# Ternary layer reordered, first normalisations moved a stage ahead, and int8 weights rounded in portions inside the third attention

## The reference

```
x = x + tanh(g_xattn[l]) * xattn_l(layernorm(x), ctx)
x = x + tanh(g_ffn[l])   * ffn_l(layernorm(x))          # l = 0..3
```

```
layer 0: routed, 16 experts, top 6, and a shared expert
layer 1: scale = mean(|w|); w_q = sign(w) * (|w| >= 0.7*scale)   for w1 (1024x256), w2 (256x1024)
         out = gelu(x @ w1_q.T + b1) @ w2_q.T + b2
layer 2: w_scale = max|w| over a row / 127; w_q = clip(round(w / w_scale), -128, 127)
         x_scale = max|x| over a token / 127; x_q likewise
         y = (x_q @ w_q.T) * x_scale * w_scale + bias
layer 3: routed, 8 experts, top 2, and a shared expert
```

## Time and profile before

| | us |
|---|---|
| median of 3 runs | 1062.74 |
| lowest, highest | 1055.58, 1065.13 |
| profiled execution | 1061.1 |
| its span, first to last instruction | 1059.3 |
| PE busy | 912.0 (86%) |
| DVE busy | 579.4 (55%) |
| ACT, POOL busy | 336.6 (32%), 417.2 (39%) |

### The profile page before, as it was taken

The page is one execution under the profiler, slowest core; times in us unless marked ns, Lnnn a source line. Parts: engine busy times, 40 slices in busy tenths (PEclk is TensorE's granted clock), DMA queues, the critical chain, the costliest instruction groups (busy, mean ns, idle before and its releaser), DMA issues. The chain is left out here.

```text
span 1059.3 us, 14410 instructions
## 1 busy us (share of the span) xinstructions
PE 912.0 (86%) x4605; PEld 702.2 (66%) x4605; DVE 579.4 (55%) x1084; ACT 336.6 (32%) x607; POOL 417.2 (39%) x328
## 2 busy tenths in 40 slices
PE   1999999697889999999949966899379788999996
PEld 1888788596656666666838965878257655565664
DVE  5567776555834444442468979666676542222221
ACT  2243443332023333333324324344133331121221
POOL 2477666203058888785322201260070005022222
PEclk9999999796679999999969977899569989899999
DMA  6411210006925544654721010000000095222210
GB/s 249 164 43 48 79 42 1 1 1 221 365 65 86 86 74 75 152 85 89 212 76 44 2 35 1 21 1 2 25 1 1 2 392 228 71 47 37 39 33 11
DMA packets 38432, 84.79 MB, mean 80 GB/s; under 512 B 9709, under 2 KB 27501, under 8 KB 35726
## 3 DMA queue, kind: packets, MB, share of 16 engines
q1 hardware_dynamic: 22190, 64.63, 17.3%
q0 software_dynamic: 16176, 19.31, 11.0%
HBM read 71.23 MB, written 20.68 MB: 87 GB/s over the span
## 5 line engine op out<-in xcount | busy, mean ns | idle before, releaser
L2391 PE MATMUL ffn_GU<-ffn_W,ffn_XTB 128*128 x252 | 91.1, 484 | 1.3 <-DVE ffn_XTB L2300 0.7
L1874 PE MATMUL ffn_GU<-ffn_W,ffn_XTB 128*128 x184 | 85.0, 605 | 0.0
L1694 POOL DMA_INDIRECT out_x<-ffn_YB,ffn_XB x23 | 35.8, 1557 | 120.2 <-DVE ffn_YB L1823 118.2
L2100 POOL DMA_INDIRECT kept_MARKED<-scratch_rows,kept_IDX x63 | 62.6, 994 | 52.0 <-DVE kept_IDX L2277 33.1
L2284 DVE TENSOR_TENSOR ffn_GB<-ffn_GU,ffn_BIAS 128x352 f32<-128x352 f32 x63 | 33.1, 525 | 87.4 <-PE ffn_GU L2391 76.2
L2391 PEld LDWEIGHTS ffn_GU<-ffn_W,ffn_XTB 128*128 128x128 f32 x252 | 43.8, 191 | 33.7 <-issue 19.4
L2422 PE MATMUL ffn_DN<-ffn_W,ffn_HT 96*128 x252 | 64.9, 380 | 0.0
L1901 PE MATMUL ffn_DN<-ffn_W,ffn_HT 128*128 (+1 forms) x248 | 58.8, 380 | 1.9 <-issue 1.2
L1812 DVE COPY ffn_XTB<-ffn_XP 128x256 f32<-128x256 f32 x23 | 9.8, 425 | 89.3 <-PE ffn_XP L1883 89.3
L2140 ACT ACTIVATE ffn_HG<-ffn_GB 128x176 f32<-128x176 f32 x63 | 22.1, 350 | 114.5 <-DVE ffn_GB L2284 81.6
L1874 PEld LDWEIGHTS ffn_GU<-ffn_W,ffn_XTB 128*128 128x128 f32 x184 | 33.1, 189 | 35.9 <-issue 33.4
(11 more groups left out here) (493 smaller groups left out, 2496.6 us busy)
## 6 DMA issues: line engine op xcount, KB each, us to landing
ffn_W<-in_f_w SPq DMA_DIRECT2D x9, 1536.0 KB, 6.6
ffn_W<-in_f_w SPq DMA_DIRECT2D x16, 608.0 KB, 17.6
attn_W<-in_L_pairs SPq DMA_DIRECT2D x8, 1088.0 KB, 4.9
scratch_rows<-in_rows_empty SPq DMA_DIRECT2D x1, 2967.0 KB, 14.2
ffn_XB<-scratch_rows SPq DMA_DIRECT2D x23, 129.0 KB, 2.1
ffn_BIAS<-in_f_bias SPq DMA_DIRECT2D x1, 2816.0 KB, 13.5
kept_STAGE<-in_f_w SPq DMA_DIRECT2D x1, 2048.0 KB, 8.3
kept_STAGE<-in_L_pairs SPq DMA_DIRECT2D x2, 768.0 KB, 5.6
```

The source lines that it names most:

```text
L1694: pool.indirect_dma_start(out[:, :], bass.IndirectOffsetOnAxis(ap=XB[:, i % NB, D:D + 1].bitcast(I32), axis=0), YB[:, i % 3, :], None, bou ...
L1874: last = pe.matmul(GU[:, m, :], x, weights(e, k * 2 * HID3 + m * HID3, HID3), start=k == 0, stop=k == KD - 1)
L2100: pool.indirect_dma_start(XB[:, i % NB, :], None, DR["rows0"][:, :], bass.IndirectOffsetOnAxis(ap=IDX[:, i:i + 1], axis=0)).then_inc(rows_ ...
L2391: last = pe.matmul(GU[:, n % 2, 0:2 * HID], XTB[:, i % 2, k * P:(k + 1) * P], flat[:, bass.ds(e * WIDTH0 + k * 2 * HID, 2 * HID)], start=k ...
```

## The change

Six things are done.

1. **First roots and normalisations in the stage ahead.** `early_root` (ACT, first four tiles) and `early_norm` (DVE, their reciprocal and four normalised tiles, put between the last two `add`) stand at the end of the first attention, `attend`, `ternary` and the third attention. At the end of the fourth attention only the root is taken early, and the int8 layer does the same for it. The following stage does the second half alone (`rooted`, `normalised`).
2. **Sums of |w|** for the ternary layer are taken by ACT inside `attend`, in four portions of 1024 elements in steps 2 to 5.
3. **Ternary layer's start**: thresholds first, LE of the first matrix ahead of the normalisation, the bias B2G ahead of WQT of the first matrix, the second matrix after `vector_low`; PE waits for half of the transposed input only.
4. **Ternary layer's rest**: every third chunk's HS_hi is rounded by ACT (`by_act`), and PE's output tiles are put between the chunks from the tenth on.
5. **Int8 weights**: `int8_weights` loads them with the third attention's first DMAs and quantises them in four portions on DVE, in the steps 5 to 8 of the third attention.
6. **Int8 layer**: weight products and transposes come first on PE, the bias is added to tiles 0 to 3 by DVE and to 4 to 7 by POOL.

```diff
+        def early_root(act, measured, rooted):
+            act.wait_ge(measured, T // 2)
+            act.activation(STD[:, 0:T // 2], MOM[:, 0:T // 2, 1], ACT.Sqrt, bias=EPS[:, 0:1]).then_inc(rooted, 1)
+
+        def early_norm(dve, rooted):
+            dve.wait_ge(rooted, 1)
+            dve.reciprocal(RSTD[:, 0:T // 2], STD[:, 0:T // 2]).then_inc(rooted, 1)
+            dve.wait_ge(rooted, 2)
+            for t in range(T // 2):
+                dve.tensor_scalar(XN[:, t, :], X[:, t, :], MOM[:, t, 0:1], RSTD[:, t:t + 1], ALU.subtract, ALU.mult)
...
@@ attend, ACT, step i
+                            if 2 <= i < 6:
+                                act.wait_ge(fetched, 16)
+                                if i > 2:
+                                    act.wait_ge(summed, i - 2)
+                                act.activation(MAGNITUDES[:, :], WT[:, i // 2 - 1, i % 2 * 1024:(i % 2 + 1) * 1024], ACT.Abs, accum_out=ASUM[:, i - 2:i - 1]).then_inc(summed, 1)
+                        early_root(act, measured, rooted)
...
@@ plain_attend, DVE
-                            measure(dve, stats, t)
+                            measure(dve, stats, t).then_inc(measured, 1)
+                            if t == T - 2 and following:
+                                early_norm(dve, rooted)
...
                             if 2 <= i:
                                 add(i - 2)
+                            if next_weights and 5 <= i <= T:
+                                next_weights["step"](dve, i - 5)
...
@@ ternary, DVE
-                        for i in range(2):
-                            dve.tensor_reduce(ASUM[:, i:i + 1], WT[:, i, :], AX, ALU.add, apply_absolute_value=True).then_inc(sums_ready, 1)
-                        nrm["vector"](dve)
-                        nrm["vector_low"](dve)
...
+                        low(0)
+                        nrm["vector"](dve)
                         dve.wait_ge(b_in, 32)
                         dve.tensor_scalar(B2G[:, :], B2[:, :], GATE[:, gate:gate + 1], None, ALU.mult).then_inc(b2_ready, 1)
+                        whole(0)
+                        nrm["vector_low"](dve)
+                        dve.wait_ge(wq_ready, 1)
+                        low(1)
+                        whole(1)
...
-                        for n in range(2 * NF):
+                        for n in range(FIRST + 1):
                             parts(n)
                         for t in range(T):
                             add(t)
+                            for n in range(FIRST + 1 + 2 * t, min(FIRST + 3 + 2 * t, 2 * NF)):
+                                parts(n)
...
@@ ternary, PE
+                        for n in range(FIRST):
+                            up(n)
+                        for t in range(T):
+                            down(t)
+                            for n in range(FIRST + 2 * t, min(FIRST + 2 * t + 2, 2 * NF)):
+                                up(n)
...
@@ int8, POOL and DVE
-                        pool.tensor_tensor(X[:, :, :], X[:, :, :], BIG[:, :].unsqueeze(1).broadcast_to((P, T, D)), ALU.add).then_inc(bias_added, 1)
+                        pool.wait_ge(x_ready, 2)
+                        pool.tensor_tensor(X[:, 4:8, :], X[:, 4:8, :], BIG[:, :].unsqueeze(1).broadcast_to((P, 4, D)), ALU.add).then_inc(bias_added, 1)
...
+                        dve.tensor_tensor(X[:, 0:4, :], X[:, 0:4, :], BIG[:, :].unsqueeze(1).broadcast_to((P, 4, D)), ALU.add).then_inc(bias_first, 1)
```

More of the change, by code:

```diff
@@ L239, in vector @@
             def vector(dve):
-                for h in range(2):
+                for h in range(normalised, 2):
                     tiles = slice(T // 2 * h, T // 2 * (h + 1))
-                    dve.wait_ge(std_ready, h + 1)
+                    if h >= rooted:
+                        dve.wait_ge(std_ready, h + 1 - rooted)
                     stats.inc(dve.reciprocal(RSTD[:, tiles], STD[:, tiles]))
@@ L255, in deviation @@
             def deviation(act):
-                for h in range(2):
+                for h in range(rooted, 2):
                     tiles = slice(T // 2 * h, T // 2 * (h + 1))
@@ L1072, in plain_attend @@
                 OP = psum(ctx, "OP", [P, 512])
-                nrm = norm(ctx, tag, [SC[:, j, :] for j in range(4)])
+                nrm = norm(ctx, tag, [SC[:, j, :] for j in range(4)], 1, normalised)
                 fetched, w_split = sem(ctx, f"{tag}_fetched"), sem(ctx, f"{tag}_weights_split")
@@ L1107, in _ @@
                         def _(sp):
+                            next_weights["load"](sp)
                             sp.dma_start(CW[:, :], A[following + "_cw"]).then_inc(fetched, 16)
@@ L1321, in ternary @@
                 NB = psum(ctx, "NB", [P, 4, 512])
-                nrm = norm(ctx, "f1", [NB[:, j, :] for j in range(4)])
+                nrm = norm(ctx, "f1", [NB[:, j, :] for j in range(4)], 1, 1)
                 b_in, fetched = sem(ctx, "b_in"), sem(ctx, "fetched")
@@ L1366, in _, with low, whole @@
                         quant.wait(dve)
-                        for i in range(2):
+                        def low(i):
                             quant.inc(dve.tensor_scalar(LE[:, :], WT[:, i, :], THR[:, 1, i:i + 1], None, ALU.is_le))
+                        def whole(i):
                             quant.wait(dve)
@@ L1425, in _, with down @@
                             last.then_inc(up_done, 1)
-                        pe.wait_ge(wq_ready, 2)
-                        for t in range(T):
+                        def down(t):
+                            if t == 0:
+                                pe.wait_ge(wq_ready, 2)
+                                pe.wait_ge(nrm["ready"], 4)
                             pe.wait_ge(h_lo, NF * (t // 4 + 1))
@@ L1434, in _, with rounded @@
                             last.then_inc(down_done, 1)
-        def int8(gate, ahead):
+                        for n in range(FIRST):
[4 more added lines that the diff above has]
+                                up(n)
+        def rounded(dve, count, dst, tmp, src, inv):
+            count.inc(dve.tensor_scalar(tmp, src, inv, MAGIC, ALU.mult, ALU.add))
+            count.wait(dve)
+            count.inc(dve.tensor_scalar(tmp, tmp, MAGIC, 127.0, ALU.subtract, ALU.min))
+            count.wait(dve)
+            return dve.tensor_scalar(dst, tmp, -128.0, None, ALU.max)
@@ L1497, in _ @@
                         nrm["deviation"](act)
+                        act.wait_ge(wt_ps, 1)
+                        act.activation(WQT[:, :, :].rearrange("p k o -> p (k o)"), WP[:, :], ACT.Copy).then_inc(wt_ready, 1)
                         for h in range(2):
@@ L1699, in _ @@
                     def _(act):
-                        for h in range(2):
-                            tiles = slice(T // 2 * h, T // 2 * (h + 1))
-                            act.activation(STD[:, tiles], MOM[:, tiles, 1], ACT.Sqrt, bias=EPS[:, 0:1]).then_inc(std_ready, 1)
+                        act.activation(STD[:, T // 2:T], MOM[:, T // 2:T, 1], ACT.Sqrt, bias=EPS[:, 0:1]).then_inc(std_ready, 1)
                         for j in (0, 2):
@@ L2491, in program @@
             HM = sbuf(mid, "HEADMASK", [P, 8])
+            ASUM = sbuf(mid, "ASUM", [P, 4])
             with ExitStack() as layer1:
```

217 lines of the change are left out of this document (127 added, 90 removed).

## The result

The changed kernel took 1049.05 us in the median of 4 runs (1046.49 to 1050.87), the kernel before 1061.53 on the same chip (1055.58 to 1065.13): a ratio of 0.9875, 95% interval 0.9841 to 0.991. The forecast was 1050.5. The total was right. Of its terms those of the int8 layer and the ternary layer came near; the attention's was too large, and those of the two expert layers were hidden by a transfer or outweighed by PE's clock, as the profile shows.

A forecast was written before the change was run, and what follows sets the result against it. No engine bounds the whole span: PE waits for DVE chains at layer heads, and DVE and PE alternate in the third attention. Terms -2.2 + 0 - 4.6 + 3.8 - 7.6 - 1.6 = -12.2 from 1062.74 give 1050.5 us, range 1043 to 1057.

The forecast's parts named there:

- First expert layer, -2.2: First expert layer's head: router product 2.4 us earlier, bounded by the routing weights' transfer; -2.2 us, range -1.1 to -2.4.
- the list would then be ready at 289.6, the weights at 289.4 to 290.5: First expert layer: when the first gather's two inputs arrive, with the weights' queue starting at most 1.1 us earlier.
- second rival: Both expert layers' heads are held by transfers: -2.2 becomes -1, -1.6 becomes 0; total -9.4, 1053.3 us; chance 0.14.
- Second attention, 0: Second attention: four portions of \|w\| on ACT, about 1.1 us each, fit its waiting for PE and cost 0.
- Ternary layer, -4.6: Ternary layer: first CAST 8.2 us earlier, partly lost to later work and interleaving; -4.6 us, -6.8 with WQT undisturbed.
- I take WQT at 4.6: Ternary layer: WQT of the first matrix takes 4.6 us beside POOL's addition, instead of 2.35 alone.
- first rival: DVE and POOL don't disturb each other: ternary -2.2 and int8 -0.9 more; total -15.3, 1047.4 us; chance 0.22.
- The interleaving costs some 3 us: Ternary layer: putting output tiles between chunks ends some 3 us later than making all chunks first.
- Third attention, +3.8: Third attention's loop: inserted int8 work 4.5 and normalisation 1.5, less 0.54 slack in four steps; +3.8 us, bounds +3 to +5.
- int8 layer, -7.6: Int8 layer: ends 7.6 us earlier, with DVE and POOL slowing each other's bias additions; -8.5 if undisturbed.
- Last layer, -1.6: Last expert layer's head: DVE's first reciprocal no longer waits for ACT's root and table load; -1.6 us.
- slower rival: Ternary layer: PE's clock stays at 0.5, the term is +16 instead of -4.6, total +9, 1071 us; chance 0.04.

The follow-up runs named there:

- second pair of profiles: The kernel before and the changed kernel, each run once more without edits: 1053.83 and 1039.22 us in the median.
- c_after: The changed kernel run once more without edits: 1039.22 us, ratio to the kernel before 0.9862.
- g_nobias: The changed kernel without POOL's bias addition in the ternary layer, save for 8 of 2048 elements: 1040.93 us, ratio to the kernel before 0.9911.
- e_best: The changed kernel with 12 chunks before the first output tile, two LE buffers with both comparisons early, and int8 work in pieces: 1033.93 us, ratio to before 0.9824.
- e_slots: The changed kernel with the third attention's int8 work cut into twelve pieces and its early normalisation moved into step 9: 1038.25 us, ratio to before 0.9873.

## Why the prediction came out right, and where it was wrong

- **First expert layer, -2.2.** The step to the list was right (2.2). The step "the list would then be ready at 289.6, the weights at 289.4 to 290.5" failed for the weights: their transfer was not issued up to 1.1 earlier, but 0.4 later after the stage's start (28.8 instead of 28.4; in the second pair of profiles 0.9 later), and landed 17.0 later as before. Before, the gather waited for the list; now it waits for this transfer, until 46.8 or later, so that 1.1 was gained in the first profile and 0.1 in c_after. This is the second rival, for this half of it.
- **Second attention, 0.** The portions on ACT took 1.07 each (1.1 was forecast) and cost nothing; -3.3 and -1.4 in the two profiles are the clock's, for which the sum had no term.
- **Ternary layer, -4.6.** Measured -3.9 and -3.7. First CAST 14.45 instead of 15.8: "I take WQT at 4.6" failed, and the first rival (no disturbance) as well, since LE lost 1.9 to POOL. The price came from the earlier trace rows, and there the waiting was taken for a slowdown. Shown one by one, DVE's two products take 1.21 and 1.53 because each waits for the end of POOL's instruction (689.88, 691.34) and then runs for 0.55; POOL's of 1.49 waits for the first of them in turn. DVE, then POOL, kernel before:

```profile
689.22 1.21 DVE L1266 TENSOR_TENSOR attn_KB_hi<-attn_KH,ffn_HEADMASK 128x512 fp32r<-128x512 f32 x1
690.36 1.53 DVE L1266 TENSOR_TENSOR attn_KB_hi<-attn_KH,ffn_HEADMASK 128x512 fp32r<-128x512 f32 x1
```

```profile
688.84 1.04 POOL L1245 TENSOR_TENSOR attn_KB_lo<-attn_KL,ffn_HEADMASK 128x512 fp32r<-128x512 f32 x1
689.85 1.49 POOL L1244 TENSOR_TENSOR attn_KB_hi<-attn_KH,ffn_HEADMASK 128x512 fp32r<-128x512 f32 x1
```

  "The interleaving costs some 3 us" held: 3.7 at equal clock, and 1.6 more by a fall of the clock that came in the two profiles of the changed kernel and in g_nobias, not in the five others with the same order. So a first CAST 1.3 earlier than forecast and an interleaving 2.3 dearer nearly cancelled. ACT's rounding: 0, as said.
- **Third attention, +3.8.** The mechanism was right, the size of the loop's term not: 2.5. The stage shows only +0.7 and +0.6, since 1.5 came back ahead of the loop, where the clock was 1.00 instead of 0.57. The slack is larger than 0.54 a step, since the idle time ahead of the addition takes up what comes late. Steps 5 to 8 take 0.8, 0.45, -0.15 and 1.45 more than the same steps before, for 1.4, 1.1, 0.9 and 2.4 of inserted work.
- **int8 layer, -7.6.** Measured -7.5. The disturbance was given to the wrong engine (DVE 1.22, POOL 3.26); the sum was the same because POOL's end was what counted in both.
- **Last layer, -1.6.** The first product came 1.6 earlier, and HF 2.3 later. What failed is that an earlier start was carried through to the end at the clock of the trace before.
- **The sum.** -12.2 was forecast, -12.5 measured (medians), and -11.3 in the second comparison. The ternary, attention and int8 terms gave -8.4 in the forecast and -10.7 and -10.6 in the profiles, the heads -3.8 and between -0.9 and +2.7. The hit is partly luck, errors that cancel: too much loss in the attention against gains in the expert layers' heads that the profiles don't show, and 3.3 and 1.4 of the clock in the second attention that no term held.

The slower rival (PE at the slow clock throughout the ternary layer, 1071; its terms add up to +8.4, not +9) didn't come, but its weak form did: a fall for about 3 us where PE waited for the eighth chunk.

## What to carry to other kernels

Work put into this loop, which hands tiles between engines, cost nothing where each piece fitted an idle time of its own place (5.8 us of work, 0 lost), and some 40% of itself when put in as four whole portions and the normalisation (2.5 us); cut it to the gaps, and put what is left behind the last consumer that waits. An earlier start of a chain is worth only what the next transfer and the clock leave of it: check the second-latest wait before the gain is booked (here the weights' transfer, which left 0.1 and 1.1 of 2.2 in the two profiles of the changed kernel). Stages are compared one by one over several profiles, since PE's clock alone moves an untouched stage by 1 to 4 us.

## What the runs showed of the hardware

- DVE and POOL exclude each other for a whole instruction where DVE's reads two SBUF tensors (WQT, 128x2048, 2.35 us; the bias addition, 128x1024, 1.22) or is a LE or CAST from SBUF (1.29, 0.42): the later one waits for the end of the other. POOL's addition of 8 elements took 2.24 behind WQT. DVE instructions with one operand in PSUM (XT_lo, four in 2.48 beside POOL's addition) don't wait.
- The granted clock is 0.50 or 1.00 at the same place of the same program in different executions: 552 to 555 us in the changed kernel. It also differs where two kernels have the same instructions: the last step of the third attention in e_best and e_slots, 0.50 and 1.00, 3.3 us apart. What sets it at these places stays open, as does the stretch of the last layer in which three engines stood still (213.75 against 207.17 for the kernel before), and the 4 us by which the first expert layer and the chain differ between kernels behind the first gather (248.0 to 252.0 from there to the end; 295.3 to 300.0 in all).
